# Experts stages of a four-layer kernel: pad stores in every second step from step 11 with rows from the counts, the second stage's sums from slot 55, two result pairs sent sooner

## The reference, cut to what matters

```python
x = x + lightning_attention(layernorm(x))    # x: [4, 512, 256] float32
x = x + ffn(layernorm(x))                    # first experts stage, "f"
x = x + attention_b(layernorm(x))
x = x + ffn(layernorm(x))                    # second experts stage, "g"

def ffn(x):                                  # 32 experts, top 8 with a threshold
    probs = softmax(x @ gate_weight.T)
    combine = top_k_weights_kept_until_0_8(probs)         # [tokens, 32]
    for w_gu, w_d, ce in experts:                         # INTER = 96
        g, u = split(x @ w_gu.T)
        out += (silu(g) * u) @ w_d.T * ce[:, None]
    return out
```

## Time and profile before

| | us |
|---|---|
| median of 3 runs | 1091.12 |
| lowest, highest | 1089.68, 1091.18 |
| the profiled execution | 1090.43 |
| its span, first to last instruction | 1088.7 |
| busy: PE, POOL | 877.9, 642.1 |
| busy: DVE, ACT | 583.0, 544.2 |
| stage f on the chip, about | 285 to 516 |
| stage g on the chip, about | 815 to 1089 |

### The profile page before, as it was taken

The page is one execution under the profiler, slowest core; times in us unless marked ns, Lnnn a source line. Parts: engine busy times, 40 slices in busy tenths (PEclk is TensorE's granted clock), DMA queues, the critical chain, the costliest instruction groups (busy, mean ns, idle before and its releaser), DMA issues. The chain is left out here.

```text
span 1088.7 us, 20645 instructions
## 1 busy us (share of the span) xinstructions
PE 877.9 (81%) x5504; PEld 665.9 (61%) x5504; DVE 583.0 (54%) x2104; ACT 544.2 (50%) x1084; POOL 642.1 (59%) x636
## 2 busy tenths in 40 slices
PE   5999998971489899999368998988758998999940
PEld 4666665641388699998233443544327887999830
DVE  4566785775373222226776488765535522222665
ACT  6333446640145455555268776766423554556520
POOL 2466648787577777775730010373754777777770
PEclk9999999995599999999679998988887999999975
DMA  9600002162578887773540110135326888778776
GB/s 335 252 1 2 1 20 91 67 240 78 168 233 301 281 267 220 222 259 123 174 136 35 34 35 35 49 121 215 116 103 200 261 303 280 227 218 255 270 243 204
DMA packets 93231, 181.64 MB, mean 167 GB/s; under 512 B 18985, under 2 KB 73788, under 8 KB 92736
## 3 DMA queue, kind: packets, MB, share of 16 engines
q1 hardware_dynamic: 68544, 114.19, 32.7%
q0 software_dynamic: 24576, 66.13, 16.7%
HBM read 96.34 MB, written 92.27 MB: 173 GB/s over the span
## 5 line engine op out<-in xcount | busy, mean ns | idle before, releaser
L1304 POOL DMA_INDIRECT result_rows<-ys,result_slots x288 | 286.6, 995 | 88.0 <-issue 81.0
L989 POOL DMA_INDIRECT expert_rows<-route_rows,index x224 | 223.0, 996 | 87.1 <-issue 68.0
L1955 ACT ACTIVATE b_probs<-ps 128x1024 f32<-128x1024 f32 x128 | 127.9, 1031 | 42.7 <-PE ps L1804 42.1
L1456 PE MATMUL ps<-w_gu,f_xts 128*128 x576 | 107.7, 331 | 3.3 <-ACT f_xts L1499 2.9
L1456 PE MATMUL ps<-w_gu,g_xts 128*128 x576 | 107.6, 330 | 2.9 <-ACT g_xts L1499 2.1
L1456 PEld LDWEIGHTS ps<-w_gu,f_xts 128*128 128x128 f32 x576 | 93.6, 193 | 4.5 <-issue 4.4
L1456 PEld LDWEIGHTS ps<-w_gu,g_xts 128*128 128x128 f32 x576 | 93.4, 193 | 4.3 <-issue 4.1
L1816 PE MATMUL ps<-b_probs,b_v_pad 128*32 128x512 f32 x512 | 78.4, 688 | 11.5 <-issue 5.4
L1549 DVE SCALAR_TENSOR_TENSOR g_h<-ps,g_xs,g_gate 128x96 f32<-128x96 f32 x144 | 39.1, 313 | 90.6 <-ACT g_gate L1506 87.7
L1549 DVE SCALAR_TENSOR_TENSOR f_h<-ps,f_xs,f_gate 128x96 f32<-128x96 f32 x144 | 39.2, 313 | 89.4 <-ACT f_gate L1506 88.3
L1517 ACT COPY ys<-ps 128x512 f32<-128x512 f32 x144 | 83.5, 580 | 1.9 <-PE ps L1475 1.9
(11 more groups left out here) (362 smaller groups left out, 1824.6 us busy)
## 6 DMA issues: line engine op xcount, KB each, us to landing
parts<-result_rows SPq DMA_DIRECT2D x32, 896.0 KB, 4.8
f_xs<-expert_rows SPq DMA_DIRECT2D x144, 160.0 KB
g_xs<-expert_rows SPq DMA_DIRECT2D x144, 160.0 KB
expert_rows<-pad_rows SPq DMA_DIRECT2D x64, 160.0 KB
w_gu<-in_Wgu SPq DMA_DIRECT2D x1, 6144.0 KB, 18.7
expert_rows<-pad_rows SPq DMA_DIRECT2D x1, 5120.0 KB, 29.9
result_rows<-ys,result_slots POOLq DMA_INDIRECT x288, 3.1
f_w_d<-in_Wdown SPq DMA_DIRECT2D x1, 4096.0 KB, 15.3
```

Source lines behind the costliest of these rows:

```text
L989: self.nc.gpsimd.indirect_dma_start(xs, bass.IndirectOffsetOnAxis(self.index[:, f, t, r:r + 1].bitcast(U32), 0), self.x_rows(f)[:, t, :], ...
L1304: self.nc.gpsimd.indirect_dma_start(self.y_dram, bass.IndirectOffsetOnAxis(self.slots[:, i, j:j + 1].bitcast(U32), 0), self.ys[:, i, j, :] ...
L1456: ins = nc.tensor.matmul(ps[:, bank_gu[u % 2], j * GU:(j + 1) * GU], xts[:, u % 2, o:o + P], w_gu[:, k, bass.ds(experts[j] * GU, GU)], sta ...
L1955: nc.scalar.activation(probs[:, u % RING, :, :], ps[:, 2 * (u % 2):2 * (u % 2) + 2, :], ACT.Exp, scale=float(HD) ** -0.5).then_inc(exp_don ...
```

## The change

- `PADS_AT` is 11 and a new `PADS_EVERY` is 2: the eight groups of four pad stores stand in SP's steps 11, 13, ... 25.
- The table `pads` is written by DVE at the end of step 12 (slot 3) and no longer in step 16 (slot 8), with its own semaphore `padded`.
- On PE and ACT the routing steps of slot 0 come ahead of the whole pair loop, so ahead of `turn(0)` and `keep_x(0)`.
- In stage g (where 18 scatters of batch 2 are done when it starts; in f it is 8) POOL sends the results of the pairs 0 and 1 between the last scatter of batch 2 and the first of batch 3. In stage f nothing changes there.
- The sums of stage g stand in DVE's slots 55, 57, ... 85 and no longer 62, 64, ... 92.
- The loads for the sums stand six steps of SP's loop behind the slot of their sum: in g in steps 61, 63, ... 91 for the slots 55, 57, ... 85; in f in steps 72, 74, 76, 78 for the slots 66, 68, 70, 72. Before, step and slot had the same number.

```diff
+            if f == B - 1:
+                dve.wait_ge(self.counted, f + 1)
+                nc.vector.tensor_scalar(self.pads[:, :], self.count[:, 0, :], -1.0, None, ALU.add).then_inc(self.padded, 1)
...
-            if final:
-                steps(nc.vector.tensor_scalar(self.pads[:, :], self.count[:, 0, :], -1.0, None, ALU.add))
-            else:
+            if not final:
...
-    PADS_AT = 17
+    PADS_AT = 11
     PADS = 4
+    PADS_EVERY = 2
...
                 if first == 0:
-                    routing.wait_tiles(sp, LAST)
+                    sp.wait_ge(routing.padded, 1)
...
-                if PADS_AT <= u < PADS_AT + E // PADS:
-                    store_pads(PADS * (u - PADS_AT), PADS)
+                nth = (u - PADS_AT) // PADS_EVERY
+                if (u - PADS_AT) % PADS_EVERY == 0 and 0 <= nth < E // PADS:
+                    store_pads(PADS * nth, PADS)
...
             wait_weights(pe)
+            for step, f in steps_at(0):
+                routing.tensor(pe, step, f, bank_route, apart=True)
             for u in range(PAIRS + FLUSH):
...
-                for step, f in steps_at(u):
+                for step, f in steps_at(u) if u > 0 else ():
                     routing.tensor(pe, step, f, bank_route, apart=True)
...
+        def early_pairs(scattered):
+            return 2 if (Routing.ALL - scattered) // 2 <= placed + 1 else 0
+
         def results_at(u, scattered, last):
 
-            left = (Routing.ALL - scattered) // 2
+            left = max((Routing.ALL - scattered) // 2, placed)
             pairs = TILES // 2 if last else TILES // 2 - LATER
-            if u == max(left, placed) + Routing.ALL // 2:
-                for v in range(pairs):
+            early = early_pairs(scattered)
+            if u == left - 1:
+                for v in range(early):
                     yield v
+            if u == left + Routing.ALL // 2:
+                for v in range(early, pairs):
+                    yield v
 
         def sums_at(u, last):
 
-            first, count = (62, NT) if last else (66, TT)
+            first, count = (55, NT) if last else (66, TT)
...
+        def loads_at(u, last):
+
+            return sums_at(u - 6, last)
```

More of the change, by code:

```diff
@@ L954, in __init__ @@
         self.chosen_ready, self.pos_ready, self.index_ready = sem("chosen_ready"), sem("pos_ready"), sem("index_ready")
-        self.counted, self.listed = sem("counted"), sem("listed")
+        self.counted, self.listed, self.padded = sem("counted"), sem("listed"), sem("padded")
         self.scattered = [sem(f"scattered{f}") for f in range(B)]
@@ L1339, in experts @@
     FLUSH = 4
-    PADS_AT = 17
+    PADS_AT = 11
     PADS = 4
+    PADS_EVERY = 2
+    assert PADS_AT + PADS_EVERY * (E // PADS - 1) < (TILES - PHASES[-1][1]) // 2
     LOADED = [COVERED[sum(t >= n for n in (2 * TT, 3 * TT, 3 * TT + TT // 2))] // 2 for t in range(NT)]
@@ L1518, in keep_result @@
                                ps[:, bank_y[u % 2], :].rearrange("p (j n) -> p j n", j=2)).then_inc(y_ready, 1)
+            for step, f in steps_at(0):
+                routing.scalar(act, step, f, bank_route)
             for u in range(PAIRS + FLUSH):
@@ L2292, in program @@
                         lambda u: scatters_at(u, scattered), lambda u: results_at(u, scattered, final),
-                        lambda u: sums_at(u, final), lambda u: sums_at(u, final), out_rows if final else None,
+                        lambda u: loads_at(u, final), lambda u: sums_at(u, final), out_rows if final else None,
                         weights_ready(use))
```

## The result

The changed kernel ran in 1109.64 us (median of 4 runs, 1106.47 to 1114.27), beside 1090.4 us for the kernel before on the same chip: a ratio of 1.0186, with a 95% interval of 1.0155 to 1.0216, or 19.2 us slower. Forecast was 1100.5 us, 9.4 slower, and a range up to 1108.5. The direction and the mechanism came out; the size is twice the forecast. The profiled run took 1106.91 us with a span of 1105.1.

A forecast was written before the change was run, and what follows sets the result against it. Loads of `parts` and DVE's sums were taken to bound the end, with PE stalled by pad stores. Stage f's -3.8 and stage g's +13.2 gave +9.4 us, 1099.8, or about 1100.5 as median; range 1094.5 to 1108.5.

The forecast's parts named there:

- Pads: Pad stores in every second SP step: PE's stalls for expert rows go, 7.5 us in f and 7.8 in g.
- Stage f, -3.8: End of stage f: PE and DVE finish at 509 to 511, POOL's landed scatters end it at 511.2, 3.8 us sooner.
- the pads' gain fails in f: Rival: SP's groups take longer beside scatters or four sum loads hold DVE; f gives 0, 1104 to 1105 us; chance 0.12.
- Routing and the two pairs: Early routing costs PE and DVE about 0.9 us in both stages; two early results put POOL 0.9 us ahead in g.
- The first sum: Stage g: its load waits for 44 pairs landed, until 993.2; pair 55 ends at 1002.4, 4.7 us later than before.
- The cycle, 10.9 us: Stage g, tiles 1 to 5: issue 1.7, landing 5.4, sum 2.6, next pair 1.2; two pairs take 10.9 us, not 5.64.
- My upper end: Stage g's sum loads: 6.4 us each time instead of 5.4, 6 us more in all.
- The rest, 17.9 us: Stage g: pairs 66 to 71 and sums 6 to 9 are DVE work in a row, 17.9 us.
- The last turns: End of stage g: three turns of 7.66 us, each a load and a sum, for sums 11, 13 and 15.
- Hidden loads: Rival in g: sums find their rows ready, POOL bounds the tail; about 1079 us, needs a 9.3 us cycle; chance 0.08.
- that rival: PE's clock falls in g: five cycles grow about 0.4 us each, pairs 66 to 71 about 5; 1107 us; chance 0.12.

The follow-up runs named there:

- a lead of four pairs: Changed kernel with stage g's sums from slot 58, their loads from step 61, and stage f's loads at their sum's step: 1080.86 us, ratio 0.9912.
- the run with the dummy turns: Changed kernel with 14 unused identity transposes on PE ahead of the waiting hidden turn in slots 57 to 69 of stage g: 1112.1 us, ratio 1.0201.
- lead of two: Changed kernel with stage g's sums from slot 56 in place of 55, their loads still from step 61: 1084.58 us, ratio 0.9963.

## Why the prediction was wrong in size

Step by step, on the profiled runs, with g counted from its start:

- **Pads.** The stall in g went, as said. Of the 7.8 us that it cost PE there, 5.1 reach the end when the pads stand alone; the rest stops at POOL's 44 pairs, which the prediction had as the bound of the first load.
- **Stage f, -3.8, was -0.3.** The step that failed is the one that put DVE's end at 509 to 511 and so let POOL set the stage's, at 511.2. POOL's last scatter moved from 506.09 to 504.87, and DVE ended at 513.86. Two terms were too good. PE was to be 6.6 us sooner (7.5 less 0.9), but DVE comes to pair 63 only 2.4 us sooner (201.1 us after the stage's first expert rows, before 203.5): it is 1.3 us behind at pair 0 and 2.8 at pair 12, and PE waits 1.63 near pair 26. With the pads alone, too, it is 1.9 behind at pair 12 and 3.5 ahead at pair 63; why the spread groups cost that much before pair 12 stays open. And the first sum, with its load behind `load(71)`, takes back 2.1 of the 2.4; it was given 1 to 3. I had "the pads' gain fails in f" as a rival, at 0.12, with both causes, SP's groups and the four loads.
- **Routing and the two pairs.** +0.9 and -0.9 forecast. Pair 2 reaches POOL 65.6 us after g's start, where at the old pace it would have been at 66.0. DVE's pair 0 comes 1.0 us later in g and 1.3 in f, but at pair 11 of g all nine kernels with both parts are 1.1 to 3.3 us behind the kernel before, and the three others are within 0.3 of it. So they cost PE more than forecast. The time doesn't show it, since POOL's 44 pairs bound the first load.
- **The first sum.** Load at 988.65, sum 0 at 993.86; counted from g's start pair 55 ends at 184.0 us, forecast 185.5. Near, and bound by POOL as said; the 44 pairs had landed 3.0 us after the start of their last scatter and not 5.1. With pads and sums both moved PE is there first; with the sums alone, on the kernel before, DVE was through with pair 54 only 179 us after g's start, and not 173, and PE was the later one.
- **The cycle, 10.9 us.** It was 11.8 in the mean of five (10.4 to 13.0): +4.5. The term that was too small is the landing, taken as 5.4 us because "the new stretch is less crowded than the old". The six loads landed in 5.2, 6.4, 7.3, 5.5, 4.9 and 6.9 us. The five behind the first, 6.2 in the mean, make 3.9 of the 4.5; the rest is the sum with the pair behind it, 4.05 us and not 3.8, less a quicker issue. My upper end, 6.4 each, held it.
- **The rest, 17.9 us.** It was 21.5: +3.6. I took pairs 66 to 71 as DVE's own work in a row. DVE waited for PE's matmuls through ACT three times there, 1.26, 1.63 and 0.71 us, 3.6 together: two pairs and a sum are 5.1 us on DVE and 5.6 on PE, so PE was the bound. The clock was a part of it, about 1 us by the run where it was 1.00 in this stretch.
- **The last turns.** 22.6 us, forecast 23.0.

In g these make 13.2 - 1.5 + 4.5 + 3.6 - 0.4 = 19.4, and 287.1 - 267.7 is 19.4. With f's -0.3 that is +19.1, beside +19.2 in the medians; the profiled pair differs by less, 16.4 in its spans, since its attention was 1.8 us shorter and the end of the first layer 0.9 sooner.

**Rivals.** Hidden loads needed a cycle under 9.3 us; the changed kernel's was 11.8, with another pair of lead most of the landing was hidden, and with a lead of four pairs all of it. The clock fell as that rival said: 1.91 us for four matmuls after four of the six waits and 1.03 a pair later, a clock of .78 in the cycles. The Trainium skill, "TensorE: Matmul & The Clock Gate", section "HAM oscillation", has this rhythm of data waits that throttle PE anew, and the trace agrees. Its consequence didn't follow here: PE's slow matmuls lay beside the next landing, where DVE never waited for them, and the price that shows is about 1 us, in the tail, where I gave 7. Why two of the four runs of the changed kernel took 1112 and 1114 us, at mean clocks of .904 and .899 against .910 for the others, stays open; the run with the dummy turns had the same spread at a higher clock in the cycles.

The range ended at 1108.5 because each case in it carried one error. Three came together: f, the landing and PE in the tail, 3.5 + 4.5 + 3.6 = 11.6 us, less 1.9 at the first sum and the last turns.

## What to carry to other kernels

Count the lead of a load not in slots but in what stands between its issue and its use on the engine that releases it. If a load's issue waits for work that stands behind the last consumer of the ring, then issue, landing and use are one chain, and one slot more of lead, here 11.8 to 7.4 us a cycle and 23 to 25 us in all, takes it apart at once: the load then lies beside the sum before it, too, and not only beside one pair more. Where a stall is removed on one engine, price the end of each stage on every engine that ends near it (in f POOL and DVE were 4 us apart), with the new waits in it, and count what the work moved ahead costs there.

## What the runs showed of the hardware

In the cycles of the changed kernel a load of `parts` (896 KB), alone behind POOL's scatters, landed in 4.9 to 7.3 us, and in 4.7 to 8.6 with its neighbour in flight (lead of two); one of four sevenths its size, alone, took 3.8 to 5.9. From the means, 3/7 of the bytes are 1.2 of 6.0 us. An estimate from that, in proportion, is that less than half of the landing (2.7 us) goes with the size here. PE's granted clock was .78 in 62 us of cycles, in which DVE waited for nothing of PE's, and .85 in the 23 us behind them, which took 1.1 us less at 1.00.
